# Attention between two FFNs: query positions kept in SBUF, one query buffer for two kinds of products, keys fetched in four pieces, and the weights phase in another order

## The reference

```python
def attention(X, Wq, Wk, Wv, Wo, We):         # B,S = 1,4096; D = 256; H = 16; DK = 16; DE = 32
    ctx = X @ We.T                            # 4096 x 32
    influence = jnp.einsum('bqe,bke->bqk', ctx, ctx)
    Q, K, V = heads(Wq), heads(Wk), heads(Wv) # 16 heads of 16 elements
    scores = jnp.einsum('bhqd,bhkd->bhqk', Q, K) * SCALE + 0.1 * influence[:, None]
    attn = jax.nn.softmax(scores, axis=-1)
    out = jnp.einsum('bhqk,bhkd->bhqd', attn, V)
    return out.transpose(0, 2, 1, 3).reshape(b, s, d) @ Wo.T

def fp4_linear(x, w):                         # the FFN's product: both sides in blocks of 16
    return jnp.einsum('bsk,nk->bsn', fp4_quant_dequant(x), fp4_quant_dequant(w))
```

## Time and profile before

| | |
|---|---|
| Median of three runs | 3794.17 us (3793.79 to 3797.96) |
| Time of the profiled execution | 3794.98 us |
| Its span in the profile | 3793.2 us |
| TensorE, products | 3656.0 us busy, 96% |
| VectorE | 3114.7 us, 82% |
| ScalarE | 2533.1 us, 67% |
| GpSimd | 1104.9 us, 29% |
| Transfers | 187.61 MB, mean 49 GB/s |

### The profile page before, as it was taken

One profiled execution on the slowest core, in us unless ns is written; L12 is line 12 of the kernel. 1 busy time (PEld: TensorE's weight loads), 2 busy tenths in 40 slices (PEclk: granted clock), 3 DMA queues, 4 the chain that ended last, 5 costly groups with the idle time before them and its releaser, 6 DMA issues. The chain is left out here.

```text
span 3793.2 us, 79235 instructions
## 1 busy us (share of the span) xinstructions
PE 3656.0 (96%) x28132; PEld 2466.6 (65%) x28132; DVE 3114.7 (82%) x5241; ACT 2533.1 (67%) x4811; POOL 1104.9 (29%) x906
## 2 busy tenths in 40 slices
PE   3998799999999999999999999999999999999799
PEld 2897466666666666666666666666666666665698
DVE  7996688888888888888888888888888888885798
ACT  4764376666777766666777666676666666766465
POOL 3990112222222222222222222121222222222597
PEclk9999799999999999999999999999999999999899
DMA  3004511212121212121212121212121212122000
GB/s 131 18 20 158 128 38 40 47 41 48 40 48 41 48 39 49 40 49 40 49 40 49 40 48 40 49 40 49 40 48 41 48 41 45 41 51 79 35 19 23
DMA packets 310556, 187.61 MB, mean 49 GB/s; under 512 B 197440, under 2 KB 240864, under 8 KB 309216
## 3 DMA queue, kind: packets, MB, share of 16 engines
q1 hardware_dynamic: 304688, 179.88, 21.3%
q10 hardware_dynamic: 5552, 3.44, 0.4%
HBM read 144.54 MB, written 33.55 MB: 47 GB/s over the span
## 5 line engine op out<-in xcount | busy, mean ns | idle before, releaser
L1313 DVE TENSOR_REDUCE tops<-coarse 128x1 f32<-128x512 f32 x4069 | 2485.1, 683 | 496.7 <-PE coarse L1200 496.5
L1302 ACT ACTIVATE x_all<-fine 128x512 f32<-128x512 f32 x4096 | 2063.0, 625 | 789.8 <-PE fine L1214 789.0
L1214 PE MATMUL fine<-query_a,key_a 64*128 64x512 f32 x4096 | 1576.2, 428 | 0.3
L1214 PE MATMUL fine<-query_b,key_b 33*128 33x512 f32 x4096 | 1493.0, 394 | 2.8 <-DMA query_b<-neg_max 2.8
L1214 PE MATMUL fine<-query_c,key_c 64*128 64x512 f32 x4096 | 1482.0, 391 | 0.0
L1200 PE MATMUL coarse<-key_a,max_query 64*128 64x512 f32 x4069 | 1432.1, 420 | 21.8 <-DMA max_query<-scratch_c_query 13.5
L1200 PEld LDWEIGHTS coarse<-key_a,max_query 64*128 64x128 f32 x4069 | 715.6, 186 | 522.8 <-DVE tops L1313 226.7
L1223 PE MATMUL o_ps<-x_all,vh 128*32 128x512 f32 x8192 | 984.8, 598 | 0.0
L1214 PEld LDWEIGHTS fine<-query_a,key_a 64*128 64x128 f32 x4096 | 753.0, 185 | 77.2 <-ACT x_all L1302 11.1
L1214 PEld LDWEIGHTS fine<-query_b,key_b 33*128 33x128 f32 x4096 | 753.5, 184 | 75.5 <-DMA query_b<-neg_max 5.6
L1214 PEld LDWEIGHTS fine<-query_c,key_c 64*128 64x128 f32 x4096 | 756.7, 185 | 42.6
(11 more groups left out here) (193 smaller groups left out, 2650.1 us busy)
## 6 DMA issues: line engine op xcount, KB each, us to landing
query_c<-scratch_c_query SPq DMA_DIRECT2D x256, 128.0 KB, 2.7
query_a<-scratch_q_hi SPq DMA_DIRECT2D x512, 32.0 KB, 1.8
query_a<-scratch_c_query SPq DMA_DIRECT2D x256, 64.0 KB, 2.0
query_b<-neg_max SPq DMA_DIRECT2D x1024, 0.5 KB, 2.0
max_query<-scratch_q_hi SPq DMA_DIRECT2D x508, 32.0 KB, 1.8
max_query<-scratch_c_query SPq DMA_DIRECT2D x254, 64.0 KB, 2.0
query_b<-scratch_q_lo SPq DMA_DIRECT2D x256, 32.0 KB, 2.4
x_all<-in_L_attn_X SPq DMA_DIRECT2D x4, 1024.0 KB, 12.4
```

The costliest lines, as they stand in the source:

```text
L1214: return pe.matmul(fine[i % 2][:, r, :], keys[rows, cols], query[rows, :], start=chunk == 0, stop=chunk == CHUNKS - 1)
L1302: act.activation(probs[:, i % RING, r, :], fine[i % 2][:, r, :], ACT.Exp).then_inc(probs_ready, 1)
L1313: dve.tensor_reduce(tops[n][:, idx // KB, idx % KB:idx % KB + 1], bank, AX.X, ALU.max).then_inc(tops_ready, 1)
```

## The change

It has four parts.

1. *Projection's stores and the scratch layout.* `q` and `k` in scratch become `[head, high or low, 16, tokens]`. A store of 128 rows so becomes one of 8 heads by 16 rows.
2. *Queries.* `query_a` and `query_c` are one buffer of all 4096 tokens each; the positions in them are loaded once at the start of the phase. `key_a` holds 32 rows of positions and 16 of high keys (`A_ROWS` 48 in place of 64); the same `query_a` serves coarse and fine products, and `max_query` is gone. `query_b` gets the low and high queries (32 rows) and the maxima, `key_b` the high and low keys. In a step SP loads the head's rows of `query_a` for step s+3 (two transfers of 16 rows) and `query_b` for s+1 (two of 32 rows).
3. *Keys.* The next head's come in four pieces, one behind `load_max` in each of four steps. SP's program is written out, with no loop.
4. *Weights phase.* The back half of `down` is done in two halves of 768 columns, the left by VectorE and the right by POOL; ScalarE rounds in halves; VectorE's order of fronts, splits and statistics is another.

```diff
--- before.py
+++ after.py
@@ weights_phase
-        scale = [scale_sb[0][:, :], scale_sb[1][:, :], small_ps[:, 384:384 + NB[2]]]
+        scale = [scale_sb[m][:, :] for m in range(3)]
+        LEFT, RIGHT = slice(0, IP), slice(IP, 2 * IP)
...
+                pool.wait_ge(step_ready, 4)
+                pool.tensor_tensor(xn[2][:, RIGHT], xn[2][:, RIGHT], step_sb[2][:, RIGHT], ALU.add).then_inc(back_chain, 1)
+                pool.wait_ge(back_chain, 5)
+                pool.tensor_tensor(xn[2][:, RIGHT], xn[2][:, RIGHT], step_sb[2][:, RIGHT], ALU.subtract).then_inc(back_chain, 1)
+                pool.wait_ge(back_chain, 6)
+                pool.tensor_tensor(blocks_of(raw[2][:, RIGHT]), blocks_of(xn[2][:, RIGHT]), spread(right_scale, IP // BLK), ALU.mult).then_inc(down_back, 1)
...
-                        pe.wait_ge(down_back, 1)
+                        pe.wait_ge(down_back, 2)
@@ projection_phase
-                            name, rows = "qk"[slot // 2], slice(slot % 2 * P, (slot % 2 + 1) * P)
-                            sp.dma_start(scratch[name + "_hi"][rows, cols], hi).then_inc(saved[n], 16)
-                            sp.dma_start(scratch[name + "_lo"][rows, cols], lo).then_inc(saved[n], 16)
+                            dst, heads = scratch["qk"[slot // 2]], slice(slot % 2 * H // 2, (slot % 2 + 1) * H // 2)
+                            for part, rows in enumerate((lo, hi) if slot < 2 else (hi, lo)):
+                                sp.dma_start(dst[heads, part, :, cols], rows).then_inc(saved[n], 16)
@@ attention_phase
-        query_a, query_b, query_c = [[sb(f"query_{part}{n}", [P, QB], F32R) for n in range(2)] for part in "abc"]
-        max_query = [sb(f"max_query{n}", [P, QB], F32R) for n in range(2)]
+        query_a, query_c = [sb(f"query_{part}", [P, T], F32R) for part in "ac"]
+        query_b = [sb(f"query_b{n}", [P, QB], F32R) for n in range(2)]
...
+        def load_heads_queries(eng, s, loaded):
+            for r in range(2):
+                eng.dma_start(query_a[half_rows(r, DE, DK), tokens(s)].bitcast(F32), scratch["q"][s // NQB, 1, :, tokens(s)]).then_inc(loaded[s % 2], 16)
...
+                def load_keys_b(n, head, r):
+                    src = scratch["k"][head].rearrange("two d t -> (two d) t")
+                    sp.dma_start(in_blocks(key_b[n][half_rows(r, 0, M_ROW), :]), every_other(src, r)).then_inc(kb_loaded[n], 16)
+
+                def load_keys_a(n, head, r):
+                    sp.dma_start(in_blocks(key_a[n][half_rows(r, DE, DK), :]), every_other(scratch["k"][head, 0], r)).then_inc(k_loaded[n], 16)
...
+                load_query_positions(sp, slice(2 * QB, T), qc_loaded[1])
+                for r in range(2):
+                    sp.dma_start(query_c[half_rows(r, 0, HALF), :].bitcast(F32), scratch["c_query"][DE:DE + HALF, :]).then_inc(qc_loaded[1], 16)
...
-                    if within(s + 3):
-                        sp.wait_ge(coarse_ready, UNITS * (s + 2))
-                        load_operand_a(sp, 1 - half, max_query, s + 3, mq_loaded)
...
+                for s in range(STEPS):
+                    step(s)
+                    head, block = divmod(s - 2, NQB)
+                    after, piece = divmod(s - 1, NQB)
+                    if 0 < after < H - 1:
+                        load_keys((after + 1) % 2, after + 1, piece)
...
-                    rows = half_rows(r, 0, HALF if chunk < CHUNKS - 1 else M_ROW + 1)
+                        rows = half_rows(r, 0, A_ROWS)
+                        keys, query = key_a[kp][rows, cols], query_a[rows, queries]
```

More of the change, by code:

```diff
@@ L910, in group_of_waves @@
             if WAVES[r][k] == "C":
-                wave.append((r, None, products[r], count))
+                wave.append((r, None, "coarse", products[r], count))
                 products[r] += 1
@@ L914, in group_of_waves @@
             else:
-                tile, chunk = divmod(tiles[r], CHUNKS)
-                wave.append((r, tile, chunk, None))
+                tile, at = divmod(tiles[r], CHUNKS)
+                wave.append((r, tile, PARTS[at], at, None))
                 tiles[r] += 1
-                if chunk == CHUNKS - 1:
-                    ended.append((tile, r))
-        waves.append(sorted(wave, key=lambda item: item[1] is None or item[2] == 0))
+        wave.sort(key=lambda item: item[1] is None or item[3] == 0)
+        ended += [(tile, r) for r, tile, what, at, order in wave if tile is not None and at == CHUNKS - 1]
+        waves.append(wave)
     return waves, ended
 GROUP_WAVES, TILES_ENDED = group_of_waves()
-UNITS_IN_GROUP = len(WAVES[0]) * 2 - 2 * GROUP * CHUNKS
+UNITS_IN_GROUP = 2 * WAVES[0].count("C")
 TILES_IN_GROUP = 2 * GROUP
@@ L929 @@
 HALF = P // 2
+A_ROWS = DE + DK
+KEY_PIECES = 4
 M_ROW = 2 * DK
@@ L1063, in _ @@
                 for n in range(2):
-                    link(pool.memset(query_b[n][:, :].bitcast(F32), 0.0))
-                for n in range(2):
-                    link(pool.memset(key_b[n][:, :].bitcast(F32), 0.0))
                     for r in range(2):
@@ L1140, in _, with step @@
+                load_query_positions(sp, slice(2 * QB, T), qc_loaded[1])
+                for r in range(2):
+                    sp.dma_start(query_c[half_rows(r, 0, HALF), :].bitcast(F32), scratch["c_query"][DE:DE + HALF, :]).then_inc(qc_loaded[1], 16)
+                load_heads_queries(sp, 2, qa_loaded)
+                for piece in range(KEY_PIECES):
+                    load_keys(1, 1, piece)
                 load_max(0, 0)
-                def step(s, half, before_last, last):
+                def step(s):
@@ L1161, in step @@
                     if within(s + 1):
-                        load_max(s + 1, 1 - half)
-                    if within(s + 3):
-                        sp.wait_ge(coarse_ready, UNITS * (s + 2))
-                        load_operand_a(sp, 1 - half, max_query, s + 3, mq_loaded)
-                step(0, 0, None, False)
-                step(1, 1, None, True)
-                for block in range(2):
-                    step(block + 2, block, (0, block), True)
-                for head in range(H - 1):
-                    with sp.Fori(0 if head else 1, NQB // 2) as i:
-                        for half in range(2):
-                            block = 2 * i + half
-                            step(sp.snap(head * NQB + block + 2), half, (head, block), True)
-                    if head + 2 < H:
-                        load_keys_a(head % 2, head + 2)
-                        load_keys_b(head % 2, head + 2)
@@ L1179, in _ @@
-                for block in range(NQB - 2):
-                    step((H - 1) * NQB + block + 2, block % 2, (H - 1, block), True)
-                    if block == 0:
-                        sp.wait_ge(v_ready, H)
-                    for dst, src, loaded in reload[block]:
-                        sp.dma_start(dst, src).then_inc(loaded, 16)
+                        load_max(s + 1, (s + 1) % 2)
+                for s in range(STEPS):
[4 more added lines that the diff above has]
+                        load_keys((after + 1) % 2, after + 1, piece)
+                    if head == H - 1:
+                        if block == 0:
+                            sp.wait_ge(v_ready, H)
+                        for dst, src, loaded in reload[block]:
+                            sp.dma_start(dst, src).then_inc(loaded, 16)
```

184 lines of the change are left out of this document (93 added, 91 removed).

## The result

The changed kernel takes 3819.62 us (median of 4 runs, 3815.74 to 3821.92) against 3794.14: a ratio of 1.0064, interval 1.0046 to 1.0081. That is slower by some 25 us. The time lies in the range given and on the side forecast, but 20 us under the 3840 and outside the likeliest case's own range of 3825 to 3866. Its profiled execution took 3815.74 us, span 3813.9.

A forecast was written before the change was run, and what follows sets the result against it. TensorE was taken to pace the attention loop, other bounds going stage by stage, with the projection's stores deciding. From 3795, gains of −15 and +59 for the stores gave 3839, written as 3840 us; range 3790 to 3866.

The forecast's parts named there:

- the likeliest case: Projection: stores of the new shape slow to about 130 GB/s; time about 3840 us, own range 3825 to 3866.
- the projection's term: Projection: the 8x16x512 stores set the pace at 17.6 us a block against TensorE's 10.60, costing +59 us.
- half of the 260 is 130 GB/s, and 121 and 138 lie around it: Projection: the new stores' rate, taken from eight engines of sixteen and rows of transfers reaching few partitions.
- The rival with eight free engines: Projection: eight engines unhindered, 197 GB/s, 12.0 us a block, +11 to +15, time 3791 to 3796; chance 0.19.
- The number of rows costs nothing: TensorE's products: 394 ns over 33 rows and 391 over 64, so 64 to 48 gives 0.
- a forecast of −0.9: Start of attention: smaller first batch of loads −1.4 us, larger second batch just covered, +0.5.
- −8.6: Attention loop: 8.6 of the 9.6 us of excess recovered at head changes, bounds −9.6 and −4.
- the keys in four pieces: Attention loop: one piece a step in place of six loads at once removes the late steps, −8.6 us.
- a rival on the side of loss: Attention loop: SP's written-out program costs only if fetching uses up some 4 us of slack a step; no chance given.
- The new wait: Weights phase: TensorE's transposition needs both halves, so VectorE waits for `d_hi` from 41.3 to 43.8, +2.5 us.
- the rivals of the term that failed: Projection's stores: unchanged 3780 us (0.15), eight free engines 3791 to 3796 (0.19), partly in step 3799 to 3826 (0.20).
- My sign of being wrong: Projection: wrong if stores of the new shape move above 200 GB/s; the time then falls to 3780 to 3795 us.

The follow-up runs named there:

- e5: Kernel before the change with products of key_a over 48 rows in place of 64, leaving sixteen rows of positions out of the scores: 3802.15 us, ratio 1.0019.
- e3: e1 with the bulk load of later queries' positions and the second head's keys moved behind the first maxima's transfers: 3789.76 us, ratio 0.9981 to the kernel before.
- e6: Kernel before the change with SP's attention loop written out, transfers and their order unchanged: 3789.18 us, ratio 0.9985.
- e4: e1 with the four pieces of the next head's keys all issued in one step: 3792.43 us, ratio 0.9991 to the kernel before.
- e12: e9 with the scales of down's left half also written to PSUM, where VectorE's last pass reads them: 3781.00 us, ratio 0.9962 to the kernel before.
- e1: Changed kernel with scratch laid out as head, row, part, token, so stores have 128 rows again: 3792.92 us, ratio 0.9992 to the kernel before.
- e9: Kernel before the change with the new weights phase, SP written out and keys in four steps: 3785.10 us, ratio 0.9970.
- e7: e6 with the six loads of the next head's keys spread over four steps: 3786.24 us, ratio 0.9977 to the kernel before.
- e8: Kernel before the change with the changed weights phase alone: 3792.93 us, ratio 0.9994.
- e10: e9 with the product of key_b and query_b over 64 rows in place of 33, added rows zero: 3781.45 us, ratio 0.9961 to the kernel before.

## Why the prediction was right, and where it wasn't

**What bounds the kernel, and the projection's term.** That the stores decide, on which side, and through which wait was right. Its size was wrong: +59 forecast, +28.7 measured. The step that failed is "half of the 260 is 130 GB/s, and 121 and 138 lie around it". Those rows are for transfers in which sixteen engines go to few partitions; the new stores are eight engines that go to many. Nor are the pieces alike: all 756 packets of 686 to 689 are under 2 KB (0.36 MB, some 500 bytes each), where the stores have rows of 2 KB, so a share over 1 at 121 GB/s need not mean engines that stand behind one another. Which of the two makes those loads slow wasn't separated. The nearest row was the old store itself: 395 × 8/16 = 197 against 193 measured. The rival with eight free engines had the rate but took 12.0 us for a block; 2.10 MB at 193 GB/s and the small stores fill that, and 2 more go in the pause and the slow start of each block's stores, which no case had.

**48 rows for 64.** "The number of rows costs nothing" was wrong, and I had priced it from the only rows that speak of it, 394 and 391 ns. The mean of a product doesn't show a cost. It lies in the clock's return at the start of attention, 9 us later than with 64 rows, and in steps that are 0.02 us longer: e5 puts both together at 6.5 us. I gave no rival to this part.

**The start of attention.** +5.7 for a forecast of −0.9. The first batch gave 0.4 us and not 1.4: it moved 1.12 MB and not 0.99, and of the 9.7 us from the first load to TensorE's first product the transfers move for some 6 only. The bulk load took some 31 us, from 437 to 468, where I had said 29; late was what stands behind it in the queues, the maxima, by 2.3 us (e3). The rest is the clock (e5).

**The loop.** −7.4 for −8.6. The late steps vanished as forecast. But "the keys in four pieces" wasn't the reason: SP written out, which I had put at 0 with a rival on the side of loss, gives most of it in the kernel of before (e6), and with 16 transfers a step the pieces bring nothing (e4). What is missing from the 8.6 is the longer undisturbed step.

**Weights phase.** −4.5 for −5.5. The new wait was seen, at 2.5 us and measured at 3.6: 0.6 is the lock that I left out of the sum as no row had the pair (e12), and the passes of 768 columns took 1.80 and not 1.72.

**The sum.** −15 + 59 was forecast, and −8.0 + 28.7 measured on the profiled executions. Two errors on opposite sides, 30 us too much for the stores and 7 us too much gain from the rest, left the forecast 23 us above the profiled execution. That the time lies in the range is owed to its width, which took in the rivals of the term that failed. My sign of being wrong was stores above 200 GB/s; the 193 measured misses it only just, although the step to 130 had failed.

**Open.** Why an undisturbed step is 23.84 us in the changed kernel and 23.87 in e1, e3 and e4, whose loops are the same but for the scratch layout (and, in e4, the time of the key loads); whether e9 really falls short of the sum of e7 and e8, by 2.4 us, which the intervals leave open; what makes the stores pause at a block's start; and what sets the spread of the clock's return, 2.6 to 7.1 us, among kernels with 64 rows.

## What to carry to other kernels

Before the layout of a scratch tensor is changed, look at the outermost dimension of each side of the stores and loads: it sets how many engines carry them, 24 to 26 GB/s each here, and a dimension order such as head, row, part keeps 128 rows at one stride. When a bound is taken from the nearest row, ask first whether it is alike in the number of engines, and only then in the number of partitions. Bulk loads go behind the small transfers that something waits for, and a sequencer that is late by a few us is worth writing out.

## What the runs showed of the hardware

- Stores of 128x512, 8x16x512 and 4x32x512, all of 256 KB in rows of 2 KB, moved at 395, 193 and 102 GB/s, at DMA shares of 1.05, 0.52 and 0.26. With rows two apart the first still moved at 404 (e1).
- Fewer rows in a product don't make it shorter (393 ns at 33 rows in e9, 390 at 64 in e10), but the kernel around it gets slower: in fourteen traces the granted clock came back 2.6 to 7.1 us after dense work began with 64 rows, and 11.5 to 17.4 with 48. In the one trace with zero rows added to a third kind of product the loop was 3.1 us shorter.
- SP's loop cost 0.8 us at a change of head against the same issues written out.
- A multiplication on POOL took 2.96 us beside a pass of VectorE with two inputs in SBUF, and 2.37 beside the same pass with one in PSUM.
